# Feed-forward head moved into the stream of attention heads, full-batch block moved in front

## The reference

```
x = x + dtw_align(ctx, layernorm(x))            # dynamic time warping against 722 context rows
x = x + moe16(layernorm(x))                     # 16 experts, top 3 per row, hidden 1024
x = x + cross_attention(ctx, layernorm(x))      # 8 heads of 64, output @ W_out + b_out
y = layernorm(x)
logits = y @ Wg.T + bg ; w = top2(softmax(logits))        # 4 experts
base = y @ Wi.T                                 # 512 -> 2048, one for all experts
lora = (y @ A[e].T) @ B[e].T                    # rank 4 for each expert
x = x + sum_e w[e] * (relu(base + lora[e]) @ Wo.T)
```

## Time and profile before

| | us |
|---|---|
| median of 3 runs | 1233.2 |
| the profiled execution | 1236.41 |
| its span | 1234.6 |
| TensorE busy | 1065.2 (86% of the span) |
| VectorE busy | 467.5 (38%) |
| ScalarE busy | 337.2 (27%) |
| GpSimd busy | 208.6 (17%) |

### The profile page before, as it was taken

How to read it: one execution, slowest core, us unless ns; L and a number is a source line. 1 busy time by engine, 2 the same in 40 slices (tenths; PEclk the granted TensorE clock), 3 DMA queues, 4 the chain that set the end, 5 groups by cost and what they waited for, 6 DMA issues and landing times. The chain is left out here.

```text
span 1234.6 us, 16867 instructions
## 1 busy us (share of the span) xinstructions
PE 1065.2 (86%) x5202; PEld 684.2 (55%) x5203; DVE 467.5 (38%) x1703; ACT 337.2 (27%) x802; POOL 208.6 (17%) x315
## 2 busy tenths in 40 slices
PE   6967579937936999999999999499999959999997
PEld 5962235523435677767767777344466544555554
DVE  6847888873560100000000000157745354112212
ACT  4424756770001222222222222143264320000000
POOL 0863021210021112111111121100000000111111
PEclk9888799968957999999999999889999958999999
DMA  8777005129305556866596566340000071000000
GB/s 295 221 162 218 1 1 179 54 97 262 102 11 197 178 180 194 308 218 195 189 329 195 193 198 192 92 137 0 1 2 1 1 254 40 1 0 1 14 14 27
DMA packets 71664, 152.79 MB, mean 124 GB/s; under 512 B 11930, under 2 KB 16162, under 8 KB 70774
## 3 DMA queue, kind: packets, MB, share of 16 engines
...
...
## 5 line engine op out<-in xcount | busy, mean ns | idle before, releaser
L1287 ACT ACTIVATE att<-phid,b 128x128 f32<-128x128 f32 x216 | 79.3, 367 | 308.0 <-PE phid L1256 308.0
L1309 DVE TENSOR_TENSOR att<-py,att 128x512 f32<-128x512 f32 x27 | 18.7, 691 | 369.1 <-PE py L1264 369.1
L1256 PEld LDWEIGHTS phid<-tiles,W 128*128 128x128 f32 x896 | 111.5, 192 | 37.4 <-issue 37.4
L1256 PEld LDWEIGHTS phid<-tiles,Wmem 128*128 128x128 f32 x832 | 105.4, 195 | 38.9 <-issue 38.9
L1256 PE MATMUL phid<-tiles,W 128*128 x896 | 114.4, 276 | 1.2 <-issue 0.3
L1256 PE MATMUL phid<-tiles,Wmem 128*128 x832 | 108.2, 279 | 5.5 <-issue 4.5
L1264 PE MATMUL py<-W,att 128*128 128x512 f32 x224 | 110.0, 593 | 0.0
L1264 PE MATMUL py<-Wmem,att 128*128 128x512 f32 x208 | 102.2, 593 | 0.0
L2082 PE MATMUL bf<-xT_f,Wmem 128*128 128x400 f32 x256 | 93.1, 519 | 0.1
L2123 PE MATMUL acc<-hs,WoT 128*128 128x400 f32 x256 | 90.6, 505 | 0.0
L2233 DVE SCALAR_TENSOR_TENSOR h<-bf,wb 128x400 f32<-128x400 f32 x64 | 32.4, 566 | 131.2 <-PE bf L2113 130.1
...
## 6 DMA issues: line engine op xcount, KB each, us to landing
...
cT<-in_ctxT SPq DMA_DIRECT2D x8, 1444.0 KB, 11.8
...
```

Source lines behind the costliest of these rows:

```text
L1256: ins = pe.matmul(ph[j % NH][:, :], W1[u][:, k, j * P:(j + 1) * P], xgT[:, bass.ds(w, 1), k * P:(k + 1) * P].rearrange("p o t -> p (o t)") ...
L1287: act.activation(hT[:, j, :], ph[j % NH][:, :], ACT.Relu, bias=b1[:, bass.ds((e + u) * HJ + j, 1)]).then_inc(relu_ok, 1)
```

## The change

The layernorm of x, its transposition, the logits and the low-rank inputs of batches 0 to 6 are made inside the stream of heads of `attend`; batch 7 remains for `feed_forward`. The expert choice is made in two halves: batches 0 to 3 in the stream (`head_parts`, group 0), batches 4 to 7 in `feed_forward` (`second_head`). The output bias is added to x by GpSimd, in front of the stream, and `add_x` adds the attention's product right to x (with the factor `few`, 1 for a batch with compacted keys and 0 otherwise). The root is no longer made on ScalarE: GpSimd raises the variance to the power -0.5. `attend_full` now stands between `experts` and `attend`. Wi is fetched in four parts during the stream, WoT in four parts at the start of `feed_forward`. The first `base_x` no longer stand ahead of the turned low-rank inputs; turning and spreading the second half stand behind `base_x(4)` and `base_x(5)`.

```diff
+        TAIL = PAIRS
+
+        def batch_at(p, first):
+            b, r = (p - first) // PB, (p - first) % PB
...
+            for b in range(B):
+                pool.wait_ge(lat_ok, b + 1)
+                pool.tensor_tensor(x_sb[:, b, :], x_sb[:, b, :], bout[:, :], ALU.add).then_inc(xb_ok, 1)
+            for b in range(NORMED):
+                pool.wait_ge(mv_ok, b + 1)
+                pool.tensor_scalar(res["rs"][:, b:b + 1], res["mv_f"][:, b, 1:2], EPS, None, ALU.add).then_inc(rs_step, 1)
+                pool.wait_ge(rs_step, b + 1)
+                pool.tensor_tensor(res["rs"][:, b:b + 1], res["rs"][:, b:b + 1], res["minus_half"][:, 0:1], ALU.pow).then_inc(rs_ok, 1)
...
+                if batch_at(p, 3 * PB) is not None:
+                    pe.wait_ge(xt_ok, batch_at(p, 3 * PB) + 1)
+                if batch_at(p, 3 * PB + 1) is not None:
+                    pe.wait_ge(lg_ok, batch_at(p, 3 * PB + 1) + 1)
...
+            def turn_x(b, i):
+                pe.wait_ge(xn_ok, b + 1)
+                if i == 0:
+                    pe.wait_ge(pt_ok[0], (2 * b + 6) if b < NORMED - 1 else PAIRS // 2)
+                for k in range(KD):
+                    ins = pe.transpose(bank[i][:, k * P:k * P + S], xn[:, b % 2, k * P:(k + 1) * P], ident[0:S, 0:S])
+                ins.then_inc(x_mm, 1)
+
+            def logits(b, i):
+                if b == 0:
+                    pe.wait_ge(w_in, 32)
+                if i == 1:
+                    pe.wait_ge(pt_ok[1], 2 * b + 6)
+                pe.wait_ge(xt_ok, b + 1)
+                for k in range(KD):
+                    ins = pe.matmul(bank[i][0:S, 0:E_L + ER], xT[:, k, b * S:(b + 1) * S], res["WgA"][:, k, :], start=k == 0, stop=k == KD - 1)
+                ins.then_inc(l_mm, 1)
...
+            def low_T():
+                pe.wait_ge(low_ok, 1)
+                pe.wait_ge(pt_ok[0], PAIRS // 2)
+                pe.wait_ge(xt_ok, NORMED - 1)
+                for b in range(HB):
+                    ins = pe.transpose(bank[0][:, b * S:(b + 1) * S], res["low"][:, b, :], ident[0:S, 0:S])
+                ins.then_inc(lt_mm, 1)
+
+            def spread_weights(k):
...
+                pe.matmul(bank[1 - k][:, 0:NH2], res["ones"][0:S, :], res["wdiag"][k].rearrange("p b s -> p (b s)"), start=True, stop=True).then_inc(wb_mm, 1)
...
+                if p < TAIL and batch_at(p, 2 * PB + 2) is not None:
+                    turn_x(batch_at(p, 2 * PB + 2), 0)
+                if p < TAIL and batch_at(p, 2 * PB + 3) is not None:
+                    logits(batch_at(p, 2 * PB + 3), 1)
+                if p == TAIL:
+                    low_T()
+                    spread_weights(0)
+                if p == TAIL + 1:
+                    spread_weights(1)
+                if p == TAIL + 2:
+                    pe.wait_ge(wb_ok[0], 1)
+                    turn_x(NORMED - 1, 1)
+                if p == TAIL + 3:
+                    pe.wait_ge(wb_ok[1], 1)
+                    logits(NORMED - 1, 0)
...
+            def keep_x(b, i):
+                act.wait_ge(x_mm, b + 1)
+                act.wait_ge(v_mm, B)
+                act.activation(xT[:, :, b * S:(b + 1) * S], bank[i][:, :].rearrange("p (k s) -> p k s", k=KD)[:, :, 0:S],
+                               ACT.Copy).then_inc(xt_ok, 1)
...
+                if p <= TAIL and batch_at(p, 2 * PB + 3) is not None:
+                    keep_x(batch_at(p, 2 * PB + 3), 0)
+                if p == EXP_AT:
+                    head.exp(act, 0)
+                if p == TAIL + 1:
+                    act.wait_ge(lt_mm, 1)
+                    act.activation(lowT[:, 0:NH2], bank[0][:, 0:NH2], ACT.Copy).then_inc(lt_ok, 1)
+                if p == TAIL + 2:
+                    act.wait_ge(wb_mm, 2)
+                    act.activation(wb[1][:, 0:NH2], bank[0][:, 0:NH2], ACT.Copy).then_inc(wb_ok[1], 1)
...
+                if p == TAIL + 2:
+                    keep_x(NORMED - 1, 1)
...
                 dve.wait_ge(w_mm, b + 1)
-                dve.tensor_tensor(att[0:S, b, :], bo[b % 2][0:S, :], bout[:, :], ALU.add).then_inc(out_ok, 1)
+                dve.wait_ge(xb_ok, b + 1)
+                dve.scalar_tensor_tensor(x_sb[:, b, :], bo[b % 2][0:S, :], few[0:S, b:b + 1], x_sb[:, b, :], ALU.mult, ALU.add).then_inc(out_ok, 1)
...
+            def moments(b):
+                dve.wait_ge(out_ok, b + 1)
+                link(dve.bn_stats(res["stats_f"][:, b, :], x_sb[:, b, :]))
+                dve.bn_aggr(res["mv_f"][:, b, :], res["stats_f"][:, b, :]).then_inc(mv_ok, 1)
+
...
+            def norm_x(b):
+                dve.wait_ge(rs_ok, b + 1)
+                dve.wait_ge(t_mm, B)
+                if b >= 2:
+                    dve.wait_ge(x_mm, b - 1)
+                dve.tensor_scalar(xn[:, b % 2, :], x_sb[:, b, :], res["mv_f"][:, b, 0:1], res["rs"][:, b:b + 1], ALU.subtract, ALU.mult).then_inc(xn_ok, 1)
...
+                if p <= TAIL and batch_at(p, 3 * PB) is not None:
+                    keep_logits(batch_at(p, 3 * PB), 1)
...
+                if batch_at(p, 2 * PB) is not None:
+                    moments(batch_at(p, 2 * PB))
                 if b >= 0 and r == 0:
                     sums_over(b)
+                if batch_at(p, 2 * PB + 1) is not None:
+                    norm_x(batch_at(p, 2 * PB + 1))
+                if p == EXP_AT - 1:
+                    dve.wait_ge(lg_ok, HB)
+                    head.largest(dve, link, 0)
+                if p == EXP_AT:
+                    head.shares(dve, link, 0)
+                if p == EXP_AT + 1:
+                    head.two_best(dve, link, 0)
+                if p == EXP_AT + 2:
+                    head.one_hot(dve, link, 0)
+                if p == EXP_AT + 3:
+                    head.low_rank(dve, 0).then_inc(low_ok, 1)
+                if p in (EXP_AT + 4, EXP_AT + 5):
+                    head.weight_diag(dve, ident, 0, p - EXP_AT - 4).then_inc(wdiag_ok, 1)
                 if b >= 0 and r == 3:
-                    add_bias(b)
...
+                    dve.tensor_copy(wb[0][:, 0:NH2], bank[1][:, 0:NH2]).then_inc(wb_ok[0], 1)
+            keep_logits(NORMED - 1, 0)
...
                 sp.dma_start(Bt[32 * i:32 * i + ER, :], io["Bt"]).then_inc(w_in, 16)
...
+            for c in range(4):
+                sp.dma_start(WoT[:, 4 * c:4 * c + 4, :], io["WoT"][4 * c * P:(4 * c + 4) * P, :].rearrange("(j p) d -> p j d", p=P)).then_inc(wo_in[c], 16)
...
+            rs = res["rs"][:, LAST:B]
+            pool.wait_ge(mv_ok, 1)
+            pool.tensor_scalar(rs, res["mv_f"][:, LAST, 1:2], EPS, None, ALU.add).then_inc(rs_step, 1)
+            pool.wait_ge(rs_step, 1)
+            pool.tensor_tensor(rs, rs, res["minus_half"][:, 0:1], ALU.pow).then_inc(rs_ok, 1)
...
+            act.wait_ge(t_mm, 1)
+            act.activation(xT[:, :, LAST * S:B * S], acc[0][:, :].rearrange("p (k s) -> p k s", k=KD)[:, :, 0:S], ACT.Copy).then_inc(t_ok, 1)
+            head.exp(act, 1)
+            act.wait_ge(lt_mm, 1)
+            act.activation(lowT[:, NT4:XT], acc[2][:, 0:NT4], ACT.Copy).then_inc(lt_ok, 1)
+            for k in range(2):
+                act.wait_ge(wb_mm, k + 1)
+                act.activation(wb[k][:, NT4:XT], acc[3 * (1 - k)][:, 0:NT4], ACT.Copy).then_inc(wb_ok, 1)
             for g in range(2):
                 act.wait_ge(acc_mm, FJ * (g + 1))
...
+            def turn_last():
+                pe.wait_ge(xn_ok, 1)
                 for k in range(KD):
-                    ins = pe.transpose(acc[2 + b % 2][:, k * P:k * P + S], xn[:, b, k * P:(k + 1) * P], ident[0:S, 0:S])
+                    ins = pe.transpose(acc[0][:, k * P:k * P + S], xn[:, LAST % 2, k * P:(k + 1) * P], ident[0:S, 0:S])
                 ins.then_inc(t_mm, 1)
...
-                pe.wait_ge(t_ok, b + 1)
+            def logits_last():
+                pe.wait_ge(t_ok, 1)
                 for k in range(KD):
-                    ins = pe.matmul(bx[0:S, b * 32:b * 32 + E_L + ER], xT[:, k, b * S:(b + 1) * S], WgA[:, k, :], start=k == 0, stop=k == KD - 1)
+                    ins = pe.matmul(acc[1][0:S, 0:E_L + ER], xT[:, k, LAST * S:B * S], res["WgA"][:, k, :], start=k == 0, stop=k == KD - 1)
                 ins.then_inc(l_mm, 1)
...
                 g, f = i // FJ, i % FJ
+                if i == 0:
+                    pe.wait_ge(res["wi_in"], 16 * KD)
+                if i >= NBK:
+                    pe.wait_ge(read2, i - NBK + 1)
                 for k in range(KD):
-                    pe.matmul(bank[i % NBK][:, 0:NT4], Wi[:, k, f * P:(f + 1) * P], xT[:, k, g * NT4:(g + 1) * NT4], start=k == 0, stop=False)
-
...
+                    pe.matmul(bank[i % NBK][:, 0:NT4], Wi[k][:, f * P:(f + 1) * P], xT[:, k, g * NT4:(g + 1) * NT4], start=k == 0, stop=False)
                 if i == 0:
-                    pe.wait_ge(lt_ok, 2)
-
-                pe.matmul(acc[(i + 2) % 4][:, 0:NT4], ones[0:S, :], wdiag[i % 2][:, :, :].rearrange("p b s -> p (b s)"), start=True, stop=True).then_inc(wb_mm, 1)
```

(37 more changed lines are left out.)

346 lines of the change are left out of this document (179 added, 167 removed).

## The result

| | before | after |
|---|---|---|
| median, us | 1233.38 (4 runs) | 1212.72 (4 runs) |
| lowest to highest | 1230.03 to 1233.56 | 1209.31 to 1215.51 |
| span of the profiled execution | 1234.6 | 1207.6 |

The changed kernel is 1.7% faster: the ratio of the times is 0.9834 with a 95% interval of 0.981 to 0.9859. The forecast of 1213 us and its sign were met. On the chip of the first group of experiments the changed kernel took 1212.86 us (5 runs), 0.9828 of the kernel before there.

The account below looks back on a forecast made before the run. TensorE was taken to bound the stream and the chain between engines the head, with a gap between. Terms -34.1 + 0.2 + 12.0 + 1.6 = -20.3 gave 1213 us against the median, 8-in-10 range 1205 to 1223.

Parts of the forecast that it names:

- Feed-forward to `down(0)`: From the start of feed-forward to `down(0)`: 56.8 us becomes 22.7, a gain of 34.1; bounds 20 to 27.
- The wait of `turn_last`: In feed-forward, behind `base_x(0)`: the turn needs batch 7's normalised rows after about 3.5 us, so 0.8 us late.
- The wait for `second(0)` and `weigh`: In feed-forward: `base_x(4)` waits for the bank that `second(0)` frees, about 0.6 us.
- The borders: Between blocks: 4.95 us gained before feed-forward, 5.1 charged for the skipped block before `attend`; together +0.2, bounds -5 to +4.
- The rival that it hides behind the read-back: In front of `attend`: the skipped block's time is hidden while x is read back, -5 us, 1208; chance 0.08.
- The stream: Stream of heads in `attend`: turns and logits 6.1 us, moments 4.7, head parts 1.2; sum +12.0, bounds +6.1 to +18.
- The rival of a stream bound by VectorE: In the stream: one more instruction or wait of about 1 us a batch before L1681, +6 us, 1219; chance 0.12.
- The clock: TensorE's clock at the start of feed-forward: +1.6 us, bounds 0 to +6; nothing charged in the stream.
- one dip of the short kind at the start of feed-forward: At feed-forward's start: 3 us at half clock, half of them lost, with a little for waits: 1.6 us.
- The slower case: In the stream: `norm_x` waiting for GpSimd blocks VectorE's queue, deciding from 5.4 us a batch; 1234 to 1238, chance 0.05.
- The ports: In the stream: GpSimd's power function holds up VectorE, at most 1.94 us for six batches, 11.6, 1225; chance 0.05.
- Turns and the clock: In the stream: more transpositions were charged nothing for the clock; the skill's contrary rule would add one short dip.

Follow-up runs that it names:

- the twelfth: The changed kernel with `attend_full` behind `attend` again and the factor of q made in `attend`: 1214.33 us against 1212.86.
- one of 4.0: The changed kernel with six more power functions a batch on GpSimd in front of the one `norm_x` waits for: 1215.54 us.
- the run with eleven: The changed kernel with eleven more power functions a batch on GpSimd in front of the one `norm_x` waits for: 1242.79 us, ratio 1.0062 to the kernel before.

## Why the prediction was right

- **Feed-forward to `down(0)`** was put at 22.7 us and is 22.9. The sum was right, but partly because its errors cancel. The wait of `turn_last` (0.8) isn't there, because GpSimd's function takes 0.56 us and not 1.67. In its place six `base_x` took 16.9 us instead of 16.1 (the first of a row is 0.2 longer), and `base` and `second` 2.8 instead of 2.3. The wait for `second(0)` and `weigh` was forecast at 0.6 and is 0.6. `second_head` had 5.8 us to spare and not 0.6: it ended 11.8 us behind the start instead of 13.4, and `low_T` was asked for at 17.6 and not at 14. That 14 was wrong by the forecast's own terms, since it has little more than five `base_x` in it (13.5) and leaves out the turn, the logits, two rounds of `base` and `second` and both waits.
- **The borders.** -4.95 at the end came as -5.0. In front of attend 5.1 were charged and 5.8 measured; leaving the block out brought 6.2. The rival that it hides behind the read-back fell.
- **The stream.** +12.0 forecast, +10.9 measured. Up to the last `sums_T` it is +12.0: 4.5 for the moments (0.75 in each of six periods), 2.1 for six turns (0.35 each, instead of 0.44), 4.1 for six logits (0.68 each), 0.3 in the two periods with head parts, and 0.9 more in the last period, where the turn of `low` and the first spread stand in front of `sums_T` and `project` waits 1.20 us instead of 0.62. The forecast counted only five logits there (3.5), took 2.6 for the turns, 4.7 for the moments and 1.2 for the head parts; its errors cancel. The tail was taken to stay as it is; it is 1.1 us shorter, since the 1.6 us that the half clock cost there before are gone. That the change took them away isn't shown: in the run with only the order changed the old tail had none of them either. That VectorE's L1681 had no slack was read rightly from one bracket of 0.31 us; the same bracket of `project`, read there too, is where the time went when the moments were moved by one place. The rival of a stream bound by VectorE did not come.
- **The clock.** +1.6 forecast, 0 measured. The step that failed is "one dip of the short kind at the start of feed-forward": in eleven of the twelve profiles with the new head there was none, and the twelfth, with 6.6 us without a product in front of it, lost 2.9 us. So with the new head the short border decides it; what the fuller tail adds isn't shown.
- **The number.** In the stages that the change touches the profiles differ by -22.2 us where -20.3 was forecast (head 0.2 off, borders 0.6, stream 1.1, clock 1.6). The other stages, mostly the one in front of the experts, make it -27.0. The medians differ by -20.7, so that 1213 was met to 0.3 us. That is closer than the terms are, and luck in part.
- **The slower case** is real, and its cover was taken too small: 2.7 us for the chain, where one of 4.0 cost the stream at most 0.4 us in one period. By the run with eleven, about 4.1 us are covered. That this is TensorE's `project` and the values of the last pair fits the timeline, and no run varies it. The 5.4 us at which the case was said to decide lie between the two chains that were tried.
- **The ports.** VectorE's `lowest` beside GpSimd's power functions kept its 0.39 us. The exclusive lock of which the Trainium skill, "SBUF — State Buffer" (SBUF: two separate sides), speaks does not show with these operands. But the skill ties it to VectorE instructions in a mode that takes both ports, or with two inputs in SBUF; `lowest` has its large input in PSUM, so that this is no test of the rule.
- **Turns and the clock.** With 24 more transpositions in front of the tail the stream's clock is 1.00. The rule of the Trainium skill that spoke against it, "TensorE: Matmul & The Clock Gate" (Part 4, PE-mode transpose), made no difference here; the transpositions stand between products, and the runs don't tell more of it.

What stays open: why the profiles differ by some us in front of the experts, why the old tail had the fall of the clock in one profile and not in the other, and why the time in front of attend differs by up to 2.3 us between kernels with the same code there.
